# Quantised cross-attention: half of the heads' weights transposed as packed bytes

## The reference

```python
q, k = _fq_sym(q, axis=-1), _fq_sym(k, axis=-1)     # 8 bits per row
v = _fq_sym(v, axis=2)
attn = einsum('bhqd,bhkd->bhqk', q, k)              # 1024 x 1024 per head
attn = softmax(attn, axis=-1)
attn = _fq_unsigned(attn, axis=-1)                  # whole numbers 0..255 times max/255
out  = einsum('bhqk,bhkd->bhqd', attn, v)
return out @ Wp + bp
```

## Time and profile before

| What | Value |
|---|---|
| Median of 3 runs | 398.72 us |
| Profiled execution | 397.78 us, span 396.0 us |
| Busy in the span | PE 310.0, DVE 340.0, ACT 316.3, POOL 124.2 us |
| Attention, VectorE's first reduction to its last | 152.8 to 340.6 us |
| DMA queue q1 | 125872 packets, 53.4% of the 16 engines' span |

### The profile page before, as it was taken

One profiled execution on the slowest core, in us unless ns is written; L12 is line 12 of the kernel. 1 busy time (PEld: TensorE's weight loads), 2 busy tenths in 40 slices (PEclk: granted clock), 3 DMA queues, 4 the chain that ended last, 5 costly groups with the idle time before them and its releaser, 6 DMA issues. The chain is left out here.

```text
span 396.0 us, 7485 instructions
## 1 busy us (share of the span) xinstructions
PE 310.0 (78%) x2589; PEld 190.8 (48%) x2589; DVE 340.0 (86%) x672; ACT 316.3 (80%) x517; POOL 124.2 (31%) x208
## 2 busy tenths in 40 slices
PE   7989998767697996677686876768776767887957
PEld 6756565422585883344353543434344444433434
DVE  4658998878778879979989999899999999688895
ACT  3776779976446588889989988899999999887861
POOL 5423525459841432200033074001200031057230
PEclk9969999699699899968989988999899998995576
DMA  8900013500200006759999998699998968800011
GB/s 266 392 2 2 2 52 106 215 1 2 92 14 2 1 4 104 142 99 186 189 160 160 188 156 140 130 168 177 174 165 147 163 130 150 120 0 17 13 35 46
DMA packets 126343, 42.68 MB, mean 108 GB/s; under 512 B 121057, under 2 KB 124769, under 8 KB 125537
## 3 DMA queue, kind: packets, MB, share of 16 engines
q1 hardware_dynamic: 125872, 41.60, 53.4%
q0 software_dynamic: 144, 0.52, 0.3%
q10 hardware_dynamic: 288, 0.07, 0.1%
HBM read 11.24 MB, written 1.05 MB: 31 GB/s over the span
## 5 line engine op out<-in xcount | busy, mean ns | idle before, releaser
L997 ACT ACTIVATE rb<-ps,eb,sq 128x1024 int16<-128x1024 f32 x128 | 154.0, 1224 | 9.3 <-DVE eb L1482 8.7
L2044 PE MATMUL ps<-ra,rb 128*128 128x512 bf16 x256 | 84.1, 415 | 42.3 <-ACT rb L997 40.8
L1482 DVE CUSTOM_DVE_ANT_0 stage<-ps,sql,sqn 128x1024 bf16<-128x1024 f32 x86 | 108.0, 1276 | 4.0 <-PE ps L2044 2.7
L1482 DVE CUSTOM_DVE_ANT_0 gs<-ps,sql,sqn 128x1024 bf16<-128x1024 f32 x42 | 53.4, 1272 | 2.9 <-PE ps L2044 2.3
L2044 PEld LDWEIGHTS ps<-ra,rb 128*128 128x128 bf16 x256 | 16.2, 100 | 61.4 <-ACT rb L997 58.0
L2071 PEld LDWEIGHTS ps<-ra,tern 128*128 128x128 f16 x624 | 25.3, 99 | 19.2 <-issue 8.4
L629 POOL TENSOR_TENSOR x<-xs,row 128x256 f32<-128x256 f32 x8 | 5.8, 728 | 77.8 <-DVE xs L1466 77.7
L997 ACT ACTIVATION_READ_ACCUMULATOR rb<-ps,eb,sq 128x1 f32 x128 | 28.2, 220 | 0.0
L2071 PE MATMUL ps<-ra,tern 128*128 128x16 f16 x624 | 26.0, 171 | 2.8 <-DVE rb L1208 2.7
L2056 PE MATMUL ps<-idh,rb 128*128 128x128 f16 x224 | 18.4, 229 | 6.7 <-ACT rb L997 4.4
L471 POOL TENSOR_SCALAR ve<-mv 128x2 f32<-128x2 f32 x7 | 1.5, 210 | 70.3 <-DVE mv L1135 70.3
(11 more groups left out here) (247 smaller groups left out, 741.5 us busy)
## 6 DMA issues: line engine op xcount, KB each, us to landing
stage<-w SPq DMA_DIRECT2D x2, 1024.0 KB, 6.5
rb<-ra SPq DMA_DIRECT2D x16, 128.0 KB, 2.9
xs<-x SPq DMA_DIRECT2D x4, 256.0 KB, 4.7
cx<-ctx_in SPq DMA_DIRECT2D x4, 256.0 KB, 4.9
stage<-w_gate SPq DMA_DIRECT2D x1, 1024.0 KB, 7.8
stage<-w_up SPq DMA_DIRECT2D x1, 1024.0 KB, 10.7
stage<-w_down SPq DMA_DIRECT2D x1, 1024.0 KB, 4.7
cx<-wide_rows SPq DMA_DIRECT2D x1, 1024.0 KB, 6.3
```

What stands on the lines that cost most here:

```text
L997: A(esc[u % E_RING], bank(2 * (u % 3), 2), ACT.Exp, bias=eb[:, u % 4:u % 4 + 1], scale=sq[:, t, h:h + 1], accum_out=es[:, t % 2, h:h + 1]) ...
L1482: V.tensor_tensor_reduce(out=unread[u % 3], in0=bank(2 * (u % 3), 2), in1=sql[:, t, h:h + 1].to_broadcast([P, NK]), scale=sqn[:, t, h:h + ...
L2044: ins = M(bank(2 * (u % 3) + hf), qz[t % 2][:, h // 2, h % 2, :], kT[:, h // 2, 512 * hf:512 * hf + 512], start=True, stop=True)
```

## The change

Heads are now of three kinds. Even heads go whole through a DMA transpose, as before (`UNPACKED`). Odd heads are packed: exp writes 1024 bytes, the byte of key pair (k, k + 128) side by side in one 16-bit word, into the first half of the buffer in `esc`; SyncE turns 128x512 words into the second half of the same buffer; GpSimd's `unpack`, three units later in its order (`UNPACK_LAG`), copies bytes to 16-bit numbers in `rT`. TensorE turns heads 12 and 15 of the last tile alone. So 26 units less go over TensorE and ScalarE; DMA turns 126 units, 63 whole and 63 packed. `b1_part` now comes every second unit.

```diff
-ON_TENSOR = (1, 4, 12, 15)
+ON_TENSOR = (12, 15)
+UNPACKED = (0, 2, 4, 6, 8, 10, 12, 14)
+UNPACK_LAG = 3
 def by_tensor(w):
-    return w >= H and w % H in ON_TENSOR
+    return w >= U - H and w % H in ON_TENSOR
+def packed(w):
+    return not by_tensor(w) and w % H not in UNPACKED
...
+        esc8 = [v.bitcast(U8)[:, 0:NK].rearrange("p (c n e) -> p c e n", e=2, n=P) for v in esc]
+        words = [v[:, 0:HF] for v in esc]
+        turned_words = [v[:, HF:F] for v in esc]
+        turned_bytes = [v.bitcast(U8)[:, NK:2 * NK].rearrange("p (c n e) -> p c e n", e=2, n=P) for v in esc]
...
             def turn(u):
                 sp.wait_ge(s_exp, u + 1)
+                if packed(u):
+                    sp.dma_start_transpose(turned_words[u % E_RING].rearrange("p (c n) -> p c n", c=T // 2),
+                                           words[u % E_RING]).then_inc(s_turned[u % R_RING], 16)
+                    return
...
+            def unpack(u):
+                pool.wait_ge(s_turned[u % R_RING], 16 * turned_by_dma(u))
+                if u >= R_RING:
+                    pool.wait_ge(s_av, u - R_RING + 1)
+                nc.gpsimd.tensor_copy(rT[u % R_RING].bitcast(I16).rearrange("p (c e n) -> p c e n", e=2, n=P),
+                                      turned_bytes[u % E_RING]).then_inc(s_unpacked, 1)
             for u in range(U + 3):
+                if UNPACK_LAG <= u < U + UNPACK_LAG and packed(u - UNPACK_LAG):
+                    unpack(u - UNPACK_LAG)
...
-                if B_FIRST <= u < B_FIRST + B_STEPS * B_PIECES:
-                    b1_part((u - B_FIRST) % B_STEPS, (u - B_FIRST) // B_STEPS)
+                if B_FIRST <= u < B_FIRST + 2 * B_STEPS * B_PIECES and u % 2 == 0:
+                    b1_part((u - B_FIRST) // 2 % B_STEPS, (u - B_FIRST) // 2 // B_STEPS)
...
+                    elif v >= 0 and packed(v):
+                        act.wait_ge(s_unpacked, unpacked(v))
...
-                    A(esc[u % E_RING], bank(2 * (u % 3), 2), ACT.Exp, ...
+                    A(esc8[u % E_RING] if packed(u) else esc[u % E_RING], bank(2 * (u % 3), 2), ACT.Exp,
...
                 if by_tensor(u):
                     pe.wait_ge(s_moved, turned_by_tensor(u))
+                elif packed(u):
+                    pe.wait_ge(s_unpacked, unpacked(u))
...
                 pe.wait_ge(o_norm, t + 1)
-                pe.wait_ge(s_moved, turned_by_tensor(min(H * (t + 1) + O_TR_LAG - TR_LAG, U - 1)))
+                if t == T - 1:
+                    pe.wait_ge(s_moved, turned_by_tensor(U - 1))
```

More of the change, by code:

```diff
@@ L110, in turned_by_dma, with unpacked @@
     return sum(not by_tensor(i) for i in range(w % R_RING, w + 1, R_RING))
+def packed(w):
+    return not by_tensor(w) and w % H not in UNPACKED
+def unpacked(w):
+    return sum(packed(i) for i in range(w + 1))
 def attended_at(u):
@@ L343, in build @@
         q_turned = [k_three, k_hat]
-        s_ps, s_bias, s_exp, s_tr, s_moved, s_av = (
-            sem(n) for n in ("s_ps", "s_bias", "s_exp", "s_tr", "s_moved", "s_av"))
+        s_ps, s_bias, s_exp, s_tr, s_moved, s_av, s_unpacked = (
+            sem(n) for n in ("s_ps", "s_bias", "s_exp", "s_tr", "s_moved", "s_av", "s_unpacked"))
         s_turned = [sem(f"s_turned{b}") for b in range(R_RING)]
@@ L996, in attention @@
                         act.wait_ge(o_norm, t - 1)
-                    A(esc[u % E_RING], bank(2 * (u % 3), 2), ACT.Exp, bias=eb[:, u % 4:u % 4 + 1], scale=sq[:, t, h:h + 1],
+                    A(esc8[u % E_RING] if packed(u) else esc[u % E_RING], bank(2 * (u % 3), 2), ACT.Exp,
+                      bias=eb[:, u % 4:u % 4 + 1], scale=sq[:, t, h:h + 1],
                       accum_out=es[:, t % 2, h:h + 1]).then_inc(s_exp, 1)
@@ L2204, in _ @@
                     scores(u)
-                if u == H + ON_TENSOR[0] + TR_LAG:
+                if u == H + O_TR_LAG:
                     pe.wait_ge(n_tr_sb, NP)
```

## The result

The changed kernel took 415.81 us (median of four runs, 412.52 to 418.35), the kernel before 398.64 beside it: a ratio of 1.0435, with an interval of 1.0355 to 1.0515. It is 4.4% slower. The forecast was 395.6 with a range of 391.0 to 402.0, so both the sign and the range were wrong. (Medians are over all runs of a kernel, while ratios leave out runs more than 1.5% above its fastest, so the first experiment, with one run left, has none.) Traces are compared by tiles and not by spans, since the attention's first reduction starts anywhere from 150.1 to 155.6 us, although all these kernels are alike up to there.

A forecast was written before the change was run, and what follows sets the result against it. VectorE was taken to bound the attention, as the last wait in most units. Terms: -5.5 us idle time and late reductions, +1.2 scalings, +1.2 clock, sum -3.1; 394.7 profiled, median 395.6, range 391.0 to 402.0.

The forecast's parts named there:

- The step that failed: SyncE's queue: issuing a half-width transpose takes 0.75 us, between 0.62 and a whole one's 1.29.
- The rival: SyncE's queue: a half transpose's issue costs as much as a whole one, +10.8 us, 409.5; chance 8%.
- It hides: SyncE's issues need 20.9 us a tile after the change, just under VectorE's time, so they add nothing.
- Removed work: 26 moves off ScalarE and 26 times eight transposes off TensorE, 15.8 us each, neither coming off the end.
- The ceiling and the gain: Attention, tiles 1 to 7: at most 8.4 us from VectorE's idle time and late reductions; 5.5 us gained.
- GpSimd's copy: Unpacking a packed head on GpSimd: 1.1 us a copy, 8.8 us a tile, hidden.
- Its cover: Slack on the path from transpose through GpSimd's copy to `attend`: 2.2 us, gone if the copy took over 3.
- 2.6 us of work plus one copy: GpSimd's normalisation queued behind head 13's unpacking fits in the some 7 us before VectorE wants it.
- VectorE's scalings: Layer norm scalings in tiles 3, 5 and 7 slowed beside GpSimd work: 1.2 us, from 0 to 5.
- the upper bound: Layer norm scalings wait for the rest of a GpSimd copy: 5.0 us, 399.4 in all; rival, chance 12%.
- The clock: TensorE's clock falls oftener, some eight more stretches, one on a projection: 1.2 us, from -2.2 to +8.
- The mark set in advance for the clock: Sign that the forecast is wrong: TensorE's mean granted clock under 0.85 over tiles 1 to 7.

The follow-up runs named there:

- the first experiment: Changed kernel with heads 1, 4, 12 and 15 of tiles 1 to 7 turned by TensorE again, other odd heads still packed: 400.93 us.
- the plain copy kernel: Changed kernel with packed heads' words carried over by a plain DMA of the same 128 KB, not transposed: 395.94 us, ratio 0.9970.
- the copies alone: Kernel before with 62 GpSimd copies of 128x1024 bytes to int16 added, awaited by nobody but GpSimd's own queue: 403.87 us, ratio 1.0157.
- pairs: Changed kernel with heads 2 and 3, 6 and 7, 10 and 11, 14 and 15 packed, each pair turned by one 128x1024 transpose: 402.48 us, ratio 1.0117.
- the kernels with pairs and no added matmuls: Changed kernel with paired heads per transpose: 402.48 us; also paddings and queries spread: 402.91; plus heads 4, 13 on TensorE: 402.86; pairs only in tiles 1, 2, 4, 6: 403.40.

## Why the prediction was wrong, point by point

**The step that failed** is "I take 0.75, near the padding DMAs (0.62), which also move 128 KB". A half transpose holds SyncE for 1.28 us (median; 1.19 at the shortest), as a whole one does (1.26; 1.23). The bounds of the step held it (0.62 to 1.29); the choice within them was wrong, because it read the wrong row as the nearest: the padding is of the same size, but of another kind, and the issue goes by the kind. At three widths the shortest issue is 1167 ns (128x256), 1188 (128x512) and 1231 (128x1024, packed or whole), against 464 for a plain DMA of as many bytes as the 128x512. With 0.59 in place of 1.28 the same kernel took 395.9 us, the forecast's time.

**The rival was there and was given 8%.** "The issue of a half transpose costs as much as a whole one" was worked out at 409.5 and came at 415.8. Its price per transpose was a little low: in tile 4 they take (25.81 - 1.31 - 1.27) / 16 = 1.45 us with what lies between them, 1.41 taken. 110 x 1.45 + 6 x 1.3 + 4 x 1.4 = 172.9 us, and 175.9 were measured. The last 3 us fit tile 7: after VectorE's 2.3 us wait for the normalised rows SyncE has caught up, and it stands without work for 3.0 us between 347.45 and 354.06. The argument against it was the padding row again, so one reading of one row decided both the forecast and the weight of its rival.

**"It hides".** The tile's need was put at 20.9 us against VectorE's 21 to 25, a margin of nearly nothing for the one number without a row. A 0.1 us error in it was 0.8 us a tile; the real one was 0.5 and made 4.

**Removed work:** half right, and of no weight. ScalarE's busy time fell by 8.1 us and not by 15.8. The 0.61 of a move's row overlaps the exp behind it: in tile 4 of the kernel before the exp starts 0.47 us after its move (255.96, 256.43), so 26 moves were worth 12.2. The other 4 are perhaps exps that stand apart and no longer overlap. TensorE's busy time rose to 130.74 at the lower clock, where 99.5 were forecast. The gain needed neither number.

**The ceiling and the gain:** the ceiling is seen, the gain is not. With SyncE free, tiles 1 and 6 took 20.09 and 20.15 us with no idle time on VectorE (22.23 and 21.27 before). But tile 4 took 1.3 us more and tiles 5 and 7 1.8 each (of which 1.0 and 0.7 are waits at the projection, at a clock of 0.66 and 0.65 over the tile), so that tiles 1 to 7 are 158.95 against 157.71, where 154.6 were forecast. The 395.9 us of that kernel agrees with the forecast's time, not with its terms; its ratio allows anything from 4.2 us faster to 1.8 slower.

**GpSimd's copy:** right in size (1.04 us) and in that it is no bound. Its cover held when the words came in time: in the plain copy kernel VectorE had whole tiles without idle time, with all copies in place. What did not fit once they were late is the normalisation behind head 13's unpacking, where "2.6 us of work plus one copy" left out that the copy may wait for its transpose: 2.3 us of VectorE's time in tile 7.

**VectorE's scalings:** taken at 1.2 us, with 0 to 5 as bounds. In the changed kernel the small operations of tiles 3, 5 and 7 grew by 1.5 us over 13.9, in the plain copy kernel by 2.2; the copies alone cost the kernel before 6.2 in all, 2.8 of it in small operations. The mechanism is the upper bound's: a scaling waits for most of a copy. The Trainium skill, "SBUF — State Buffer", "Who interferes with whom", says of VectorE's two-port mode and GpSimd that one blocks the other for the whole instruction. The rows of 287.30 agree that the scaling waits for the copy; that which of the two issues first decides can't be read from them, they are 0.02 us apart. The forecast gave this 12%. How much a run pays depends on which scalings meet a copy, and it pays in what follows too.

**The clock:** taken at 1.2 us with eight more stretches; the mean of a tile was 0.62 to 0.77. With pairs the clock was nearly as low and 13 us were back, so it was not what held the changed kernel. The place that the forecast named for its cost, the projection, was right: in the kernels with pairs and no added matmuls VectorE waits 0.7 to 1.8 us at one in each layer norm tile, where 1.1 was taken for a single one. The mark set in advance for the clock (a mean under 0.85 over tiles 1 to 7) was passed and would by itself have pointed to the wrong cause; the mark for a half transpose (over 1.0 us) pointed to the right one.

## What to carry to other kernels

Work off every queue that the change lengthens as a sum per tile, issue times included, before asking what the relieved engines gain. A price that no row shows is read from the row of the same kind of instruction, not from the one of the same size, and where the margin is as thin as here the flat price is the forecast. If bytes are to be halved, halve the number of instructions: two heads in one transpose took back 13 of the 17 us that one each had lost. And where an engine is one queue, what stands behind a wait is late with it, as the layer norm was on GpSimd.

## What the runs showed of the hardware

The issue of a DMA transpose from SyncE hardly depends on its width between these three: 1167 ns for 128x256, 1188 for 128x512, 1231 for 128x1024 at the shortest. Only its landing follows the size (2.3, 2.4 and 3.0 us at the shortest). A plain DMA of 128 KB held the same queue for 464 ns at the shortest and 589 in the median.

A VectorE scaling of 128x256 that meets a GpSimd copy of 1.04 us takes 1.21 us in place of 0.35, while the custom reduction of 128x1024 beside such copies takes no longer (means of 1271 to 1278 ns in all kernels, with and without copies).

At the lower level of TensorE's clock the two fp32 matmuls of a projection take 1.20 us and not 0.68, and two score matmuls 1.06 and not 0.61. VectorE waited for the scores behind it, 0.7 to 1.8 us in each layer norm tile of the kernels with pairs and no added matmuls.
